# The short last key tile laid three times over the partitions, its products 96 rows and columns wide, and its low half given to VectorE

## The reference

```python
x   = layer_norm(ctx);  lat = layer_norm(_layernorm(x))     # cut
q   = lat @ Wq                                # 1024 queries of each batch
kv  = concatenate([ctx_normed, lat]) @ Wkv    # 154 + 1024 = 1178 keys
dots = einsum('bhid,bhjd->bhij', q, k) * scale
attn = softmax(dots)                          # over the 1178 keys
out  = einsum('bhij,bhjd->bhid', attn, v) @ Wout
x = x + out;   x = x + experts(_layernorm(x)) # top 1 of 8 experts, silu
```

## Time and profile before

| what | value |
|---|---|
| runs | 2363.96, 2368.19, 2369.15 us |
| profiled execution | 2368.87 us, its span 2367.1 us |
| clock granted to PE, mean | 0.961 |
| prologue and chunks of BEFORE | to about 100 us |
| heads 0 to 63, with four times the output projection | about 100 to 1970 us |
| experts | about 1970 to 2367 us |
| PE busy | 2139.2 us, 90% of the span |
| DVE, ACT, POOL busy | 1571.5, 1496.7, 1384.6 us |

### The profile page before, as it was taken

How to read it: one execution, slowest core, us unless ns; L and a number is a source line. 1 busy time by engine, 2 the same in 40 slices (tenths; PEclk the granted TensorE clock), 3 DMA queues, 4 the chain that set the end, 5 groups by cost and what they waited for, 6 DMA issues and landing times. The chain is left out here.

```text
span 2367.1 us, 65364 instructions
## 1 busy us (share of the span) xinstructions
PE 2139.2 (90%) x26836; PEld 1448.6 (61%) x26836; DVE 1571.5 (66%) x2914; ACT 1496.7 (63%) x1812; POOL 1384.6 (58%) x759
## 2 busy tenths in 40 slices
PE   2799999999999999999999999999999985689997
PEld 2366666666666666666666665766666665567775
DVE  7677777775777777757777777577777733564343
ACT  4277777774777777747767777477777763275554
POOL 2177667772766777726767776277776653343332
PEclk9699999999999999999999999999999986599999
DMA  4111111111111111111111111111111114341110
GB/s 153 29 40 31 35 30 31 35 35 51 31 36 30 31 38 33 40 43 35 30 31 38 32 36 35 47 31 30 40 31 35 30 55 161 98 132 32 40 40 22
DMA packets 66966, 107.26 MB, mean 45 GB/s; under 512 B 10593, under 2 KB 36885, under 8 KB 66549
## 3 DMA queue, kind: packets, MB, share of 16 engines
q1 hardware_dynamic: 62933, 93.76, 15.0%
q0 software_dynamic: 3744, 9.31, 1.2%
HBM read 40.39 MB, written 9.31 MB: 21 GB/s over the span
## 5 line engine op out<-in xcount | busy, mean ns | idle before, releaser
L421 POOL TENSOR_TENSOR probs_split<-probs,probs_split 128x1024 f16<-128x1024 f32 (+1 forms) x576 | 1222.5, 2128 | 653.2 <-ACT probs_split L496 646.7
L489 ACT ACTIVATE probs<-score 128x1024 f32<-128x1024 f32 (+1 forms) x640 | 655.1, 1024 | 495.2 <-PE score L705 494.4
L595 DVE TENSOR_REDUCE max_parts<-aux 128x1 f32<-128x512 f32 x1024 | 685.4, 688 | 168.0 <-PE aux L705 163.1
L496 ACT ACTIVATE probs_split<-score 128x1024 f16<-128x1024 f32 (+1 forms) x640 | 651.2, 1018 | 0.0
L779 PE MATMUL acc<-values,probs_split 128*128 128x65 f16 x5120 | 578.9, 193 | 3.6 <-POOL probs_split L421 3.5
L780 PE MATMUL acc<-values,probs_split 128*128 128x64 f16 x5120 | 578.8, 194 | 0.0
L781 PE MATMUL acc<-values,probs_split 128*128 128x65 f16 x5120 | 576.3, 192 | 0.0
L779 PEld LDWEIGHTS acc<-values,probs_split 128*128 128x128 f16 x5120 | 475.2, 96 | 104.7 <-issue 68.4
L705 PE MATMUL aux<-k_high,q_both 128*128 128x512 f16 (+1 forms) x1536 | 460.7, 334 | 68.8 <-DVE max_parts L595 49.5
L780 PEld LDWEIGHTS acc<-values,probs_split 128*128 128x128 f16 x5120 | 473.3, 97 | 61.2 <-issue 0.3
L705 PE MATMUL score<-q_both,k_high 128*128 128x512 f16 (+1 forms) x1280 | 487.4, 381 | 5.7 <-ACT probs_split L496 2.8
(11 more groups left out here) (163 smaller groups left out, 2277.8 us busy)
## 6 DMA issues: line engine op xcount, KB each, us to landing
k_high<-raw SPq DMA_DIRECT2D x128, 147.2 KB, 2.5
q_both<-raw SPq DMA_DIRECT2D x128, 128.0 KB, 2.4
zx_high<-in_L_ffn_W SPq DMA_DIRECT2D x16, 1024.0 KB, 5.4
k_low<-raw SPq DMA_DIRECT2D x64, 147.2 KB, 2.4
q_max<-raw SPq DMA_DIRECT2D x64, 128.0 KB, 2.4
att_rows<-in_x SPq DMA_DIRECT2D x4, 1024.0 KB, 8.7
x_res<-in_x SPq DMA_DIRECT2D x32, 128.0 KB, 2.2
x<-x_tile SPq DMA_DIRECT2D x32, 128.0 KB, 1.7
```

Source lines behind the costliest of these rows:

```text
L421: nc.gpsimd.tensor_tensor(out=low[0:r, :], in0=prob(h, j)[0:r, :], in1=high[0:r, :], op=ALU.subtract)\
L489: nc.scalar.activation(prob(h, j)[0:r, :], score[j % 2][0:r, :], ACT.Exp, scale=SCALE)\
L496: nc.scalar.activation(halves(h, j)[0][0:r, :], score[j % 2][0:r, :], ACT.Exp, scale=SCALE)\
L595: nc.vector.tensor_reduce(max_parts[g % 2][:, t, c:c + 1], bank[:, :], AX.X, ALU.max)\
```

## The change

Tile 9's 26 keys are written at partitions 0, 32 and 64, with zeros between, so the tile is 96 rows high (COPIES x COPY). Its scores are made with 96 columns of weights. Its values are high halves in rows 0 to 25, low halves in rows 32 to 57 and again high halves in rows 64 to 89; its probabilities in `probs_split` are high halves in the first two copies, and in the third DVE writes the low halves over them. One product per query tile then holds all three terms, and `weigh` of tile 9 has 8 products of 96 rows in place of 24 of 26 rows. POOL now makes the low half of tile 0 and no longer that of tile 9, DVE that of tile 9 (32 partitions) and no longer that of tile 0. The `turn` product takes 128 columns of weights (`neg_max` is padded with zeros) in place of 8. `arrange` has 2 more transfers, `arrange_low` 1 more, of 64 x 2 x 26 elements. In the prologue `zc` is filled in pieces, with 4 copies by DVE and more small memsets.

```diff
 def key_rows(j):
-    return TAIL if j == JT - 1 else P
+    return COPIES * COPY if j == JT - 1 else P
-LOW_ON_VECTOR = (0,)
+LOW_ON_VECTOR = (JT - 1,)
...
-        neg_max = sb("neg_max", [P, NT], F32)
+        neg_max = sb("neg_max", [P, P], F32)
...
+        def copies(keys):
+            return keys[:, N + P:WIDE].rearrange("p (m c) -> p m c", c=COPY)[:, :, 0:TAIL]
+        def tail_of(keys):
+            return keys[DH:P, N + P:KEYS].unsqueeze(1).to_broadcast([DH, COPIES - 1, TAIL])
...
+                for half in (slice(0, DH), slice(DH, P)):
+                    sp.dma_start(copies(keys)[half, 1:COPIES, :], tail_of(raw[0])).then_inc(arranged, 16)
...
-                sp.dma_start(k_low[g % 2][0:DH, :], raw[1][DH:P, :]).then_inc(low_arranged, 16)
+                sp.dma_start(k_low[g % 2][0:DH, 0:KEYS], raw[1][DH:P, :]).then_inc(low_arranged, 16)
+                sp.dma_start(copies(k_low[g % 2])[0:DH, 1:COPIES, :], tail_of(raw[1])).then_inc(low_arranged, 16)
...
+                if b == 0:
+                    dve.wait_ge(z_low, 2)
+                    for w in range(2):
+                        at = zc[w][:, :, :].rearrange("p k (b c) -> p k b c", c=CW)
+                        for copy in range(1, COPIES):
+                            last = nc.vector.tensor_copy(at[:, :, :, P + copy * COPY:P + copy * COPY + TAIL],
+                                                         at[:, :, :, P:C])
...
-                    nc.vector.tensor_tensor(out=value_half(g, chunk[2], 1), in0=value_bank(bank, chunk[2]),
-                                            in1=value_half(g, chunk[2], 0), op=ALU.subtract).then_inc(aux_done, 1)
+                    high, low = [value_half(g, chunk[2], half) for half in range(2)]
+                    made = value_bank(bank, chunk[2])
+                    if chunk[2] == len(VALUE_TILES) - 1:
+                        second = high[COPY:2 * COPY, 1]
+                        nc.vector.tensor_tensor(out=second, in0=made[COPY:2 * COPY, 1], in1=second, op=ALU.subtract)
+                        high, low, made = [a[:, 0:1] for a in (high, low, made)]
+                    nc.vector.tensor_tensor(out=low, in0=made, in1=high, op=ALU.subtract).then_inc(aux_done, 1)
...
                 if j in LOW_ON_VECTOR:
+                    rows = slice(2 * COPY, 3 * COPY)
+                    high = halves(h, j)[0][rows, :]
                     wait_high(dve, h, j)
-                    nc.vector.tensor_tensor(out=low[0:r, :], in0=prob(h, j)[0:r, :], in1=high[0:r, :],
+                    nc.vector.tensor_tensor(out=high, in0=prob(h, j)[rows, :], in1=high,
                                             op=ALU.subtract).then_inc(low_on_vector, 1)
...
-                    last = nc.tensor.transpose(bank[0:NT, 0:P], neg_max[:, :], ident[:, :])
+                    last = nc.tensor.transpose(bank[:, 0:P], neg_max[:, :], ident[:, :])
...
+                copied = j == JT - 1
...
-                    nc.tensor.matmul(out, high, value[:, 0:DH + 1], start=(j == 0 and q == 0), stop=False)
+                    last = nc.tensor.matmul(out, high, value[:, 0:DH + 1], start=(j == 0 and q == 0),
+                                            stop=(copied and q == NT // 2 - 1))
+                    if copied:
+                        continue
```

More of the change, by code:

```diff
@@ L467, in affine @@
                     act.wait_ge(z_affine, 2 * group + i + 1)
-                    src = probs[i][:, :].rearrange("p (k c) -> p k c", k=KD)[:, :, 0:cols]
-                    nc.scalar.activation(dst(0, i, cols), src, ACT.Copy).then_inc(z_high, 1)
+                    src = probs[i][:, :].rearrange("p (k c) -> p k c", k=KD)
+                    for part, to in dst(0, i, cols):
+                        last = nc.scalar.activation(to, src[:, :, part], ACT.Copy)
+                    last.then_inc(z_high, 1)
             act.wait_ge(ones_ready, 1)
@@ L520, in _ @@
             for i in range(2):
-                nc.vector.memset(k_low[i][DH:DH + 1, :], 1.0)
-                nc.vector.memset(zc[i][:, :, CT:CT + P - TAIL], 0.0)
+                nc.vector.memset(k_low[i][:, N + P:WIDE], 0.0)
+                nc.vector.memset(k_low[i][DH:DH + 1, 0:N + P], 1.0)
+                for k in range(KD):
+                    nc.vector.memset(zc[i][:, k, :].rearrange("p (b c) -> p b c", c=CW)[:, :, C:CW], 0.0)
+            for i in range(SETS):
+                nc.vector.memset(k_high[i][:, N + P:WIDE], 0.0)
+            nc.vector.memset(neg_max[:, :], 0.0)
             for i in range(2):
-                nc.vector.memset(values[i][:, :, :, DH:DH + 2], 1.0)
+                nc.vector.memset(values[i][:, :, 0:JT - 1, DH:DH + 2], 1.0)
+                nc.vector.memset(values[i][:, :, JT - 1, DH:DH + 2], 0.0)
             nc.vector.memset(eps_square[:, :], EPS * EPS)
@@ L528, in _ @@
             dve.wait_ge(z_step, 1)
+            for i in range(2):
+                nc.vector.memset(copies(k_low[i])[DH:DH + 1], 1.0)
+                for copy in (0, 2):
+                    last = nc.vector.memset(values[i][copy * COPY:copy * COPY + TAIL, :, JT - 1, DH:DH + 1], 1.0)
+            last.then_inc(ones_ready, 1)
             dve.wait_ge(ln_turned, 1)
@@ L557, in split @@
                     dve.wait_ge(z_high, 2 * group + i + 1)
-                    nc.vector.tensor_tensor(out=dst(1, i, cols),
-                                            in0=probs[i][:, :].rearrange("p (k c) -> p k c", k=KD)[:, :, 0:cols],
-                                            in1=dst(0, i, cols), op=ALU.subtract).then_inc(z_low, 1)
+                    src = probs[i][:, :].rearrange("p (k c) -> p k c", k=KD)
+                    for (part, to), (_, high) in zip(dst(1, i, cols), dst(0, i, cols)):
+                        last = nc.vector.tensor_tensor(out=to, in0=src[:, :, part], in1=high, op=ALU.subtract)
+                    last.then_inc(z_low, 1)
             dve.wait_ge(x_loaded[0], 32)
@@ L778, in weigh @@
                     high, low = [half[0:r, t * P:t * P + P] for half in halves(h, j)]
[L779 removed]
+                    last = nc.tensor.matmul(out, high, value[:, 0:DH + 1], start=(j == 0 and q == 0),
+                                            stop=(copied and q == NT // 2 - 1))
+                    if copied:
+                        continue
                     nc.tensor.matmul(out[:, 0:DH], high, value[:, DH + 2:VROW], start=False, stop=False)
[L781 to L782 removed]
+                    last = nc.tensor.matmul(out, low, value[:, 0:DH + 1], start=False, stop=False)
                 last.then_inc(av_done, 1)
```

50 lines of the change are left out of this document (31 added, 19 removed).

## The result

| | before | changed | ratio, 95% interval |
|---|---|---|---|
| median (us) | 2368.67 (2363.96 to 2370.05, 4 runs) | 2265.77 (2264.63 to 2271.33, 4 runs) | 0.9574 (0.9553 to 0.9594) |
| profiled execution, its span (us) | 2368.87, 2367.1 | 2265.58, 2263.9 | |

The change makes the kernel 102.9 us faster, and 103.2 by the spans of the two profiled executions. The forecast was 2267 us, in a range of 2255 to 2296. All executions timed here are of one state, but for `width_64` and `width_72`, which were timed once each and whose state is not known.

A forecast was written before the change was run, and what follows sets the result against it. PE was taken as the bound: its own pace plus one wait for DVE per head. 61 heads x (1.27 + 0.45) = 104.9, plus 1.3 + 1.9 - 3.2 - 2.4, is 102.5 off 2368.87: forecast 2267 us, range 2255 to 2296.

The forecast's parts named there:

- The changes of shape: PE's ways into and out of tile 9's scores (0.42 us) and step 9's products (0.38) become free: 0.79 us per head gained.
- PE's pace: PE's own time between products: changes of shape 0.79 plus products taken out 0.49, together 1.27 us per head gained.
- rival that 96 columns are not full: Array still changes shape or the load shows: tile 9's scores keep their 0.42 us per head, time 2293; chance 0.10.
- The products: Tile 9's products in step 9 go from 24 to 8: 16 x 0.030 = 0.49 us per head gained.
- DVE's order: Moving DVE's low-half subtraction ahead of step 7's maximum shortens PE's wait at step 8: mean 0.45 us per head gained.
- The turn at 0: Step 5's `turn` loads 128 weight columns, not 8; hidden by the wait for DVE's values: cost 0, exposed up to 10 us.
- The transfers at 0: `arrange` ends 1.28 us later, but PE asks for the data with 1.7 us of cover: cost 0.
- rival *slower: Slow `arrange` copies make PE wait; above about 2.5 us extra per transfer the kernel is slower, 2427 at 3 us; chance 0.04.
- The row of maxima: PE wants this transfer 0.40 us earlier in step 7; five late heads and one more wait 0.40 longer: -2.4 us.
- The prologue: Three more transfer issues ahead of head 0 cost 1.9 us, DVE's extra pieces and copies 1.3: -3.2 us.
- The end: In head 63 POOL starts with tile 0 in an earlier gap and tile 8 is ready 1.6 us earlier; with shorter `weigh` +1.9.
- the rest of head 0: Head 0, without a full step 8 pattern, was counted as a gain of 1.3 us.

The follow-up runs named there:

- `width_64`: The kernel before with tile 9 zero-padded to 64 rows and columns, all 24 products, no copies, low halves in their old places: 2375.63 us in one execution.
- `width_72`: The kernel before with tile 9 zero-padded to 72 rows and columns, all 24 products, no copies, low halves in their old places: 2324.72 us in one execution.
- `width_96`: The kernel before with tile 9 zero-padded to 96 rows and columns, all 24 products, no copies, low halves in their old places: 2324.18 us.
- `products_8`: The kernel before with 8 of tile 9's 24 products, still of 26 rows, leaving out the low-half terms: 2336.57 us.
- `low_places_before`: The changed kernel with tile 0's low half back on DVE behind step 7 and tile 9's back on POOL: 2300.85 us.
- `low9_max7`: The changed kernel with DVE's low half of tile 9 one place later, behind step 7's maximum: 2251.22 us.
- `low9_v7`: The changed kernel with DVE's low half of tile 9 moved behind step 7's values: 2287.44 us.

## Why the prediction was right

**What bounds the kernel: right.** PE's own distances and the waits for DVE gave 1.63 us in each of 58 heads, 94.5 of the 103.2 us of span.

**The changes of shape, 0.79 us per head: right, shown.** The distances of rows and columns are the full ones in the changed kernel. `width_96` gained 42.9 us by them alone, under the 0.79 x 64 = 50.6 of PE's pace; the waits for DVE's maxima are 4.6 us longer there and those for the row of maxima 2.2. The median distance from turn to turn is 0.73 us shorter than before, and 0.77 shorter than with 64 rows. The rival that 96 columns are not full is out; had the tile stood on 64 partitions, it would have been right.

**The products, 0.49 us per head: right, shown** by `products_8`, 0.48 us per head and 30.5 in all, against 30.7.

**DVE's order, 0.45 us per head: the mechanism right, the size 0.08 too large.** The wait moved as written out, from the third chunk to the first two, and halved less: 0.68 for 0.56 in the one kind of head, 0.46 for 0.40 in the other. The term at fault is the start of the maximum behind the subtraction. I let it start 0.07 before the subtraction's end (787.78 for 787.85); the rows have it 0.03 behind (748.10 + 1.22 = 749.32, start 749.35). In the earlier trace rows the next one starts at 790.25, before the end at 790.32; this did not carry over, and why is open. So the whole stretch on DVE is 0.1 later, and (1.72 - 1.63) x 58 = 5.2 us are missing. That the order has an effect at all is shown by `low_places_before`, and that the wait for ACT was behind what PE still waited for the maxima, by `low9_max7`, where 8.6 us of it become 0.9. Not foreseen was the link between the terms: without the new order the shorter steps would have made the old wait longer (1.01 and 0.68 for 0.92 and 0.60).

**The turn at 0: right for this kernel.** Its wait for the values in step 5 is still there. **The transfers at 0: right,** no wait, and the rows show a cover of 2.1 us in the one kind of head, where 1.7 were forecast, and 2.7 in the other. The 0.64 per issue that I used holds for the six in most heads. The rival *slower* was summed wrongly: two transfers of 1.7 us extra each use up the cover of 1.7 and cost the whole gain of 1.7 per head, so the bound is 1.7 us and not 2.5, and at 3 us each the kernel would be 2 x 3 - 1.7 - 1.7 = 2.6 us per head slower, 166 in 64, and not 60. Its chance of 0.04 went by the landing times, and the copies landed 2.0 us after their issue in the median.

**The row of maxima, -2.4: wrong, it gave 3.7 us.** I let the late landings of the kernel before come again and cost more. The changed kernel has 3 waits of 0.8 us in all, against 5 of 2.6, and the five heads that these made longer are 3.7 us shorter. How many come late changes from one profile to the next: the five profiles with the old transfers have 1 to 8 such waits, 0.3 to 6.6 us, the seven with the copies none to 4, at most 1.6 us. `products_8`, with the same transfers as the kernel before, had 1 of 0.3, so how much of the 3.7 belongs to the change and how much to chance stays open.

**The prologue, -3.2: the cause right, the size too large.** In these two profiles the first turn is only 0.5 us later. The other profiles show more. The wait on the last transfer is 1.01 to 1.03 us in all five with the old transfers and 2.71 to 2.74 in the six with three more, so the 1.7 (forecast 1.9) is no chance. The first turn comes at 93.4 to 95.4 us in the five and at 95.6 to 96.3 in the six, 1.3 us later in the mean.

**The end, +1.9: 0.8 came of it.** Measured from the last turn, POOL's last subtraction ends 1.6 us earlier, as forecast, and that although it takes 1.0 us more beside DVE's, which was not foreseen; it is the clash that `low9_v7` shows 62 times. But from POOL's end to the first division it is now 1.81 us in place of 0.92. The forecast left out that POOL's last tile is now tile 8, and that PE has the 24 products of tile 8 and those of tile 9 still to do behind it, where it had those of tile 9 alone.

**The heads with an output projection** were counted like the others: three at 1.72 each, and they gave 2.5 us together.

**The sum.** By the spans the measured gain is 103.2 us and the forecast's is 102.5, but its parts are not met as closely. Forecast too high were the common heads by 5.1 us, those with an output projection by 2.7, head 61 by 0.5 and the end by 1.1. Forecast too low were the row of maxima by 6.1, what stands ahead of step 5 of head 0 by 3.2, the rest of head 0 by 0.3 (1.6 for 1.3), and the stretch behind the heads, for which it had nothing, by 0.5. So 9.4 stood against 10.1, and that the total came within 1 us is luck. The two large terms, 1.27 of PE's pace and 0.45 of the order, are right by themselves within 0.09.

## What to carry to other kernels

Where a small tile alternates with full ones, read the distance between the starts of the products, not their lengths: if it grows by a fixed step at each way in and out, try the tile wider: past the boundary it cost nothing on the array here, and it let copies of the tile do several products in one. An engine that works in order pays for each instruction that waits with everything queued behind it: put the one that waits for the slowest partner behind the work that others want first, and try its places one at a time, since one place too far cost 36 us here (`low9_v7` against `low9_max7`). When a bounding engine is made faster, price again the waits that it has already: here they grew from 0.92 and 0.60 us to 1.01 and 0.68.

## What the runs showed that I had not expected

- The 0.10 us step has its boundary above 64 rows and columns: 64 pays, 72 and 96 do not.
- Loads of 64, 72 and 96 columns take longer, 106, 111 and 121 ns, than one of 128, 98 ns; one of 26 takes 90. It was hidden.
- When a DVE subtraction with both inputs in SBUF and one of POOL overlap, the one that starts later is longer: POOL takes 5.25 us for two tiles instead of 4.18, and in head 62 DVE 2.20 where it takes 1.22.
- In most profiles nearly all heads of a kind are alike to 0.02 us from turn to turn. The few with a late small transfer and the heads with an output projection make most of what differs between profiles of like kernels.
